# A selective scan and an expert layer on one core: batch 1 routed as one group, tables and rows of zeros moved between the expert slots, a new plan of lagging sums, weights of three experts asked for at once

## The reference, cut to what matters

```python
h = layernorm(x) * (1 + ca) + sa
# scan: x, z, B, C, delta are projections of h; u = silu(conv(x))
def step(h, inp):                      # per channel and state
    dA = exp(dt * A); h = dA * h + (dt * u) * B
    return h, (h * C).sum(-1)
y = (y + u * D) * silu(z)
x = x + ga * (y @ Wout.T + bout)
h = layernorm(x) * (1 + cb) + sb
logits = h @ gate; w, idx = top_k(logits, 2); w = softmax(w)
out = sum over the 2 experts e of w_e * (silu(h @ w0[e]) * (h @ w1[e])) @ wo[e]
x = x + gb * out
```

## Time and profile before

| | |
|---|---|
| median of three runs | 850.11 us |
| profiled execution, its own time | 850.03 us |
| span of that execution | 848.2 us |
| TensorE matmul busy | 737.5 us (87%) |
| VectorE busy | 626.6 us (74%) |
| GpSimd busy | 513.4 us (61%) |
| ScalarE busy | 340.2 us (40%) |
| scan groups end (last sum on TensorE) | 557.0 us |
| first hidden of an expert slot | 600.6 us |

### The profile page before, as it was taken

How to read it: one execution, slowest core, us unless ns; L and a number is a source line. 1 busy time by engine, 2 the same in 40 slices (tenths; PEclk the granted TensorE clock), 3 DMA queues, 4 the chain that set the end, 5 groups by cost and what they waited for, 6 DMA issues and landing times. The chain is left out here.

```text
span 848.2 us, 9598 instructions
## 1 busy us (share of the span) xinstructions
PE 737.5 (87%) x2292; PEld 370.5 (44%) x2293; DVE 626.6 (74%) x840; ACT 340.2 (40%) x387; POOL 513.4 (61%) x271
## 2 busy tenths in 40 slices
PE   5799998888797887878989878986699999999994
PEld 2444343233232332324535323465366666666663
DVE  4478889999899998999999898846444444444442
ACT  0776966456453543545445475311111111111110
POOL 1013233999999999999999898947522222222222
PEclk9999999999999999999999987997599999999998
DMA  9354645866667666676759968567662322222220
GB/s 282 98 158 148 186 158 148 205 183 175 174 158 195 176 175 181 175 188 168 207 159 238 231 138 244 143 238 244 202 203 45 49 45 34 49 46 38 46 30 0
DMA packets 62296, 126.41 MB, mean 149 GB/s; under 512 B 11898, under 2 KB 33850, under 8 KB 62140
## 3 DMA queue, kind: packets, MB, share of 16 engines
q1 hardware_dynamic: 50468, 116.12, 50.0%
q0 software_dynamic: 7152, 8.48, 5.7%
q10 hardware_dynamic: 4648, 1.48, 0.7%
HBM read 98.08 MB, written 24.69 MB: 145 GB/s over the span
## 5 line engine op out<-in xcount | busy, mean ns | idle before, releaser
L1630 POOL TENSOR_TENSOR pool<-pool,hT 128x1024 f32<-128x1024 f32 x101 | 235.8, 2355 | 15.8 <-PE PS L664 15.8
L664 PE MATMUL PS<-pool,ident 128*128 128x512 f32 x404 | 206.3, 637 | 31.0 <-POOL pool L1630 30.2
L1028 ACT ACTIVATE PS<-pool,negA 128x1024 f32<-128x1024 f32 x128 | 143.1, 1118 | 168.3 <-DVE pool L1338 168.3
L1714 POOL DMA_INDIRECT out<-uT,ptab x39 | 60.6, 1555 | 169.1 <-DVE uT L1565 157.9
L1338 DVE TENSOR_TENSOR_SCAN pool<-PS,pool 128x1024 f32<-128x1024 f32 x64 | 143.0, 2270 | 3.4 <-ACT PS L1028 3.4
L849 PE MATMUL PS<-pool,uT 128*128 (+1 forms) x312 | 145.3, 610 | 0.0
L664 PEld LDWEIGHTS PS<-pool,ident 128*128 128x128 f32 x404 | 75.8, 198 | 118.4 <-issue 59.3
L646 PE MATMUL PS<-pool 96*128 96x512 bf16 x256 | 80.8, 398 | 27.9 <-DVE wz_sb L1326 12.0
L1539 DVE TENSOR_TENSOR uT<-uT,PS 128x512 f32<-128x512 f32 x39 | 26.9, 689 | 88.4 <-PE PS L849 85.6
L1654 POOL TENSOR_TENSOR spread<-spread,pool 128x1024 f32<-128x1024 f32 x32 | 75.4, 2355 | 15.3 <-ACT spread L1034 15.3
L849 PEld LDWEIGHTS PS<-pool,uT 128*128 128x128 f32 x312 | 58.3, 197 | 59.0 <-issue 59.0
(11 more groups left out here) (197 smaller groups left out, 867.3 us busy)
## 6 DMA issues: line engine op xcount, KB each, us to landing
hT<-C_scratch SPq DMA_DIRECT2D x128, 512.0 KB, 5.3
pool<-in_w SPq DMA_DIRECT2D x16, 512.0 KB
uT<-expert_in_scratch SPq DMA_DIRECT2D x39, 130.5 KB
Y<-Y SPq DMA_DIRECT2D x32, 128.0 KB, 2.4
C_scratch<-Y SPq DMA_DIRECT2D x8, 512.0 KB, 2.6
pool<-du_scratch SPq DMA_DIRECT2D x8, 512.0 KB, 6.1
Y<-in_wo SPq DMA_DIRECT2D x8, 512.0 KB
expert_in_scratch<-zrow SPq DMA_DIRECT2D x16, 130.5 KB, 5.8
```

Source lines behind the costliest of these rows:

```text
L664: m = pe.matmul(PS[:, 6 + half, :], ident[:, :], prod_k[:, HF * half:HF * half + HF], start=False, stop=k == DS - 1)
L1028: act.activation(pair(2 * (k % 2)).unsqueeze(1), delta[:, chunk_at(g2, r), :], ACT.Exp, scale=decay[:, bass.ds(g2 * (2 * DS) + n, 1)]).the ...
L1630: gp.tensor_tensor(to, hst[:, k % HR, :], crep[k % RC], ALU.mult).then_inc(prod_done, 1)
L1714: gp.indirect_dma_start(out=out, out_offset=bass.IndirectOffsetOnAxis(ap=ptab[:, slot:slot + 1], axis=0), in_=yo[:, slot % 2, :], in_offse ...
```

## The change

It has five parts.

1. `blocks_behind` follows a table, `CATCH_UP`, of the k at which two sums are made. In group 7 the four transposes are made in two pairs (k = 0 and 1), so that the sums begin at k = 2; ScalarE's evacuations stand two each at k = 4 and 5. `first_logits` is one piece at k = 12. `ranks(0)` moves ahead of the last two sums, all `turned_back` behind them.
2. Batch 1 is one group of 8 tiles: one `pick`, `weights`, `ranks` and `place_of`, and 16 sends in a row. `rstd_of(2)` and `rstd_of(3)` stand behind 10 and 15 sends of batch 0 where it was 7 and 13.
3. The tables of later slots are made by VectorE in three pieces, behind `leave` of slots 0, 1 and 2, no longer ahead of slot 0.
4. ScalarE's eight stores of zeros stand in iterations 2 to 5, no longer 0 to 3.
5. SyncE asks for the weights of experts 0 to 2 behind the scan (nine loads, no longer twelve) and for expert e+1's behind the rows of slot e, for e = 2 to 6.

```diff
-GROUPS = ((0, NTB), (NTB, NTB + TQ), (NTB + TQ, NT))
+GROUPS = ((0, NTB), (NTB, NT))
...
             sp.wait_ge(gated, NG - 1)
-            for e in range(CH):
+            for e in range(3):
                 w0_of(e)
                 w1_of(e)
                 wo_of(e)
-            sp.wait_ge(gated, NG)
...
-                if e in (1, 2, 3, 4):
-                    w0_of(e + 3)
-                    if e == 4:
-                        w1_of(e + 3)
-                    wo_of(e + 3)
+                if 2 <= e < NE - 1:
+                    w0_of(e + 1)
+                    if e + 1 < CH or e + 1 == NE - 1:
+                        w1_of(e + 1)
+                    wo_of(e + 1)
...
+            CATCH_UP = {0: (), 2: (4, 6), TQ: (6, 8, 10, 11)}
...
+            def blocks_behind(g2, r, pieces, last):
+                made, behind = 0, len(pieces)
+                sums_at = [0] * behind + [1] * (DS - behind)
+                for k in CATCH_UP[behind]:
+                    sums_at[k] += 1
+                for k in range(DS):
+                    next_front(g2, r, k, last)
+                    if k < behind:
+                        pieces[k]()
+                    if last and k == DS - LAG:
+                        first_logits()
+                    for _ in range(sums_at[k]):
+                        if made == 0:
+                            pair_read(2 * g2 + r)
+                        if last and made == DS - 2:
+                            ranks(0)
+                        back(g2, r, made, prod_at(DS * (2 * g2 + r) + made))
+                        made += 1
...
+            def turned_pair(i):
+                turned_in(2 * i)
+                turned_in(2 * i + 1)
+
+            blocks_behind(NB + 1, 1, [lambda i=i: turned_pair(i) for i in range(2)], True)
+            for j in range(NTB // 2):
+                turned_back(j)
...
-                if g == CH + 3 and k in range(LAG, LAG + NTB // 2):
-                    take_turned(k - LAG)
+                if g == CH + 3 and k in (LAG, LAG + 1):
+                    take_turned(2 * (k - LAG))
+                    take_turned(2 * (k - LAG) + 1)
...
-            act.wait_ge(known, 2)
-            for s2 in range(2):
+            for s2 in range(NE // 2):
                 for r in range(2):
                     take_rows(s2 + 1, r)
                     silu_h(s2 + r, 1 - r)
-                    tail(4 * s2 + 2 * r)
-                    tail(4 * s2 + 2 * r + 1)
-            with act.Fori(2, SPAIRS) as s2:
+                    if s2 in (1, 2):
+                        if s2 == 1 and r == 0:
+                            act.wait_ge(known, 2)
+                        tail(4 * (s2 - 1) + 2 * r)
+                        tail(4 * (s2 - 1) + 2 * r + 1)
+            with act.Fori(NE // 2, SPAIRS) as s2:
...
+            residual(NTB, NTB + TQ)
+            normal_h2(NTB, NTB + TQ)
+            residual(NTB + TQ, NT)
+            normal_h2(NTB + TQ, NT)
             pick(1)
             weights(1)
             place_of(1)
...
-            dve.wait_ge(c_over, 1)
             dve.wait_ge(regated, 1)
...
+            def slots_of(s2, between):
                 for r in range(2):
                     take_inter(s2, r)
                     noted_of(s2 + 1, r)
                     gate_h(s2 + r, 1 - r)
                     leave(s2, r)
+                    if between:
+                        between.pop(0)()
+
+            between = [count_slots, expert_of_slots, rows_of_slots]
+            slots_of(0, between)
+            slots_of(1, between)
+            with dve.Fori(2, SPAIRS) as s2:
+                slots_of(s2, None)
...
-            send(0, slice(0, 7))
+            send(0, slice(0, 10))
             rstd_of(2)
-            send(0, slice(7, 13))
+            send(0, slice(10, 15))
             rstd_of(3)
-            send(0, slice(13, 16))
+            send(0, slice(15, 16))
...
             for q in range(1, NQ):
                 gp.wait_ge(placed, q + 1)
-                send(q, slice(0, 2 * TQ))
+                send(q, slice(0, 2 * NTB))
```

More of the change, by code:

```diff
@@ L711, in turned_back, with first_logits @@
                 m.then_inc(t2_mm, 1)
-            def first_logits(tiles):
-                for t in tiles:
-                    if t == 0:
-                        pe.wait_ge(dbu_done, 1 + NG * OWN)
-                        pe.wait_ge(spread_in, NG * len(SHARED))
-                        pe.wait_ge(t1_done, NTB)
+            def first_logits():
+                pe.wait_ge(dbu_done, 1 + NG * OWN)
+                pe.wait_ge(spread_in, NG * len(SHARED))
+                pe.wait_ge(t1_done, NTB)
+                for t in range(NTB):
                     for k in range(KD):
@@ L722, in first_logits, with ranks @@
                     m.then_inc(g_mm, 1)
+            def ranks(q):
+                first, end = GROUPS[q]
+                n = end - first
+                pe.wait_ge(tables, 1)
+                pe.wait_ge(picked, q + 1)
+                for i in range(n + (q in (0, NQ - 1))):
+                    to = PS[:, r_bank(q), P + NE * i:P + NE * i + NE]
+                    parts = [(ones[:, :], ohs[:, first + j, :]) for j in range(i)]
+                    if q:
+                        parts.append((ones[:, :], sums[:, q, :]))
+                    if i < n:
+                        parts.append((tri[:, :], ohs[:, first + i, :]))
+                    for j, (w, rhs) in enumerate(parts):
+                        m = pe.matmul(to, w, rhs, start=j == 0, stop=j == len(parts) - 1)
+                m.then_inc(rank_mm, 1)
             def next_front(g2, r, k, last):
@@ L772, in _ @@
             blocks_behind(NB + 1, 0, [lambda t=t: outward_y(t) for t in range(TQ, NTB)], False)
-            blocks_behind(NB + 1, 1, [lambda j=j: turned_in(j) for j in range(NTB // 2)], True)
-            turned_back(2)
-            turned_back(3)
+            def turned_pair(i):
[4 more added lines that the diff above has]
+                turned_back(j)
             def turn_h2(t):
@@ L796, in logits @@
                 m.then_inc(g_mm, 1)
-            def ranks(q):
-                first, end = GROUPS[q]
-                n = end - first
-                pe.wait_ge(tables, 1)
-                pe.wait_ge(picked, q + 1)
-                for i in range(n + (q in (0, NQ - 1))):
-                    to = PS[:, r_bank(q), P + NE * i:P + NE * i + NE]
-                    parts = [(ones[:, :], ohs[:, first + j, :]) for j in range(i)]
-                    if q:
-                        parts.append((ones[:, :], sums[:, q, :]))
-                    if i < n:
-                        parts.append((tri[:, :], ohs[:, first + i, :]))
-                    for j, (w, rhs) in enumerate(parts):
-                        m = pe.matmul(to, w, rhs, start=j == 0, stop=j == len(parts) - 1)
-                m.then_inc(rank_mm, 1)
             def scored(q):
@@ L820, in scored @@
                 logits(q, end - 1)
-            ranks(0)
             for t in range(NTB, NT):
@@ L1130, in gap_exp @@
                 act.activation(w12[:, 1, tiles], w12[:, 0, tiles], ACT.Exp).then_inc(ex_done, 1)
-            take_rows2(0)
-            take_rows2(1)
             gap_exp(0)
             leave(NG // 2 - 1, 1)
-            take_rows2(2)
-            take_rows2(3)
+            for j in range(NTB // 2):
+                take_rows2(j)
             for q in range(1, NQ):
@@ L1471, in gate_y, with residual @@
                 dve.tensor_tensor(uT[:, c, :], uT[:, c, :], szT[:, c, :], ALU.mult).then_inc(gated, 1)
-            def residual(q):
-                first, end = GROUPS[q]
+            def residual(first, end):
                 added_y(first)
@@ L1481, in residual, with normal_h2 @@
                     gathered(t)
-            def normal_h2(q):
-                for t in range(*GROUPS[q]):
+            def normal_h2(first, end):
+                for t in range(first, end):
                     centre(t)
-                for t in range(*GROUPS[q]):
+                for t in range(first, end):
                     h2_of(t)
@@ L1575, in _ @@
             gate_h(0, 0)
-            with dve.Fori(0, SPAIRS) as s2:
+            def slots_of(s2, between):
                 for r in range(2):
```

74 lines of the change are left out of this document (31 added, 43 removed).

## The result

The changed kernel took 860.84 us median (858.08 to 862.98, four runs), beside 849.75 us for the kernel before in the same comparison: a ratio of 1.0122, 95% interval 1.0073 to 1.0171. Its profiled execution took 861.73 us, with a span of 859.9 us, 11.7 us more than before. The prediction was 860.0 us with a range of 853.5 to 865.0.

A forecast was written before the change was run, and what follows sets the result against it. TensorE was taken to bound the slots (30% of the span), never waiting from the second slot on. Terms 0 - 0.5 + 2.5 + 0 + 5.5 + 2.5 = +10.0 on 850.03 gave 860.0 us, range 853.5 to 865.0.

The forecast's parts named there:

- The scan's last group: End of the scan: earlier sums but a later front leave GpSimd's input unchanged, about 0, ends -3.5 and +2.5 us.
- the first send stays where it was: Scan to routing: batch 0's rows still wait for four transposes and evacuations behind the last sum; no shift.
- signs of being wrong: Slots without a hole after slot 1, last scan sum over 3 us from 557.0, or a weights hole before slot 2.
- the scan gains: Rival at the scan: early sums free GpSimd, everything up to slot 8 comes 3.5 us earlier, 856.5 us; chance 0.12.
- both waits and a late scan: Rival: GpSimd's input 2.5 us late and both clock drops cost 3.25 us, 864.0 us; chance 0.10.
- Batch 1 as one group: Outward of slot 1: sends start earlier but the last lands at 620.1; start 622.6 against 623.11, -0.5 us.
- The clock: TensorE behind the holes before outward of slot 1 and slot 8: lower granted clock costs 2.5 us each.
- Tables: VectorE between slots: three pieces of 1.2 to 1.6 us, covered by TensorE's hidden except the first, counted elsewhere; 0.
- weights: Expert 3's loads follow slot 2's rows, take 4.5 us and arrive in time; later experts have over 8 us; 0.
- Zeros: Before slot 8: its rows wait for the later stores of zeros, so TensorE stands 5.5 us, ends 4.5 and 6.5.
- Only the sends don't hold: Rival: slot 2's hidden starts about 611.9, not 619.67, while slot 8's hole and clock drop remain; 850.2 us; chance 0.08.
- The early start wins: Rival: the 7.8 us between slots 0 and 2 kept, zeros in time, no hole at slot 8; 842.2 us; chance 0.05.

The follow-up runs named there:

- early zeros: The changed kernel with the zeros' row numbers computed ahead of slot 0 and the eight stores of zeros back in iterations 0 to 3; ratio 1.0141.
- part 1 alone: The kernel before with only the new scan plan (paired transposes, logits in one piece, ranks(0) ahead of the last two sums); ratio 1.0018.
- the version with tables, early buffers and early zeros: The kernel before with later slots' tables made between slots and output buffers freed before batch 1's sends, zeros left in iterations 0 to 3; ratio 0.9943.
- the group alone: The kernel before with only batch 1 routed as one group of 8 tiles, 16 sends in a row, rstd behind 10 and 15 sends; ratio 1.0033.
- part 1 undone: The changed kernel with the old scan plan put back (four single transposes, logits in three parts, batch 0's ranks behind the sums); ratio 1.0146.
- the tables alone: The kernel before with only the tables of later slots made in three pieces behind slots 0, 1 and 2; ratio 0.9963.
- both edits: The changed kernel with output buffers freed before batch 1's sends, and the stores of zeros back in iterations 0 to 3; ratio 1.0106.

## Why the prediction was right

**The sum** was +10.0 and is +11.7; the two holes and the two clock drops are where they were said to be, and behind what they were said to be behind. That the total is so close is in part luck: errors of +2.6 and +0.5 at the first hole stand against -0.7 and -0.6 at the second.

**The scan's last group (about 0).** The step "the first send stays where it was" failed: it came at 565.58, not 561.64. One of the prediction's own signs of being wrong came with it: the last sum of the scan ended at about 561.4, more than 3 us from 557.0. GpSimd's last product ended at 554.06 here and at 552.51 before; the first send followed 11.5 us later, and 9.1 before. Those 2.4 us are the plan's own: GpSimd's idle time in front of the first send is 8.8 us in every profile with the old plan, and 11.2 in four of the five with the new one (9.5 with early zeros). TensorE's timeline of the changed kernel shows where they come from, the last sums and the sums ahead of them:

```profile
550.54 6.25 PE L665 MATMUL PS<-Y,ident 128*128 128x512 f32 x8
557.74 3.68 PE L665 MATMUL PS<-pool,ident 128*128 128x512 f32 x8
```

Eight matmuls that take 3.68 us in the second row took 6.25 in the first, behind the logits in one piece: TensorE lags behind GpSimd's products at a low clock (0.80 over 545 to 562, 0.99 before). With early zeros the same eight took 5.10 and the delay is shorter. No run takes the logits or the clock apart, so this is read from the five profiles and not tested. The prediction looked for the plan's price at GpSimd's input and not at TensorE's sums. The other 1.5 us, by which GpSimd's last product was late, can't be told from the spread of that point (549.8 to 556.3 us in the five profiles with the new plan, 549.4 to 555.4 with the old). The time of part 1 alone can't be told from none. The rival "the scan gains" is excluded by the late first send, "both waits and a late scan" came true in its late scan, but the clock drops cost 3.0 and 1.9 us, not 3.25 each, and the time is 860.84 us, not 864.0.

**Batch 1 as one group (-0.5 at slot 1; it is +2.1).** The distance from the first send of batch 0 to that of the last group was put 2.9 us shorter and is 4.1 shorter (35.24 against 39.31); the late scan of 3.9 us takes all of it, so the sends start at 600.82 instead of 598.0. The last of them starts at 619.87, not 617.5, and has landed 3.2 us later, not 2.6: the wait ends at 623.1 where 620.1 was said. What stands behind the wait was put at 2.4 us and took 2.2.

**The clock (+2.5 twice)** is +3.0 and +1.9: the drop behind the hole of 7.5 us costs more than behind that of 4.8.

**Tables (0) and weights (0).** In the change they cost nothing in the sum beyond `count_slots`, which is in its first term. The weights do show: slot 3's rows, asked for at 605.04 behind expert 3's loads, were turned at 613.51, after an idle time of TensorE of 1.21 us, but TensorE stood until 625.33 all the same. That both lie in the shadow of the sends is argued, since no run took one of them out of the changed kernel; alone in the kernel before, tables gained 0.37% and weights cost 0.23%.

**Zeros (+5.5; it is +4.8).** From the issue of the last pair to the turn of slot 8 it took 7.5 us (650.56 to 658.07) where 8.0 was said. The two transfers took 2.92 and 2.25 us against 2.7 and 2.95 in the sum. The figure of the Trainium skill ("DMA: Bandwidth & Descriptors", Anatomy of one DMA), fitted there for DMAs that GpSimd issues, is an estimated 2.3 us for these 134 KB. The trace agrees for the rows (2.25) and not for the zeros (2.92), and the hole that follows from it, 4.5 us, is nearer to the measured 4.8 than mine.

**Rivals.** "Only the sends don't hold" fell: the sends hold even with the buffers given free early. "The scan gains" fell with the first send. "The early start wins" asked for sends that don't hold and zeros in time; the change has neither, and the version with tables, early buffers and early zeros, which has both, is faster than before.

## What to carry to other kernels

Fewer, larger groups save fixed steps (3.5 us in the group alone) and lengthen the block that one in-order queue must issue: look for what stands behind that block, and who waits for it. Removing a wait on a buffer helps only if the instruction that empties the buffer isn't queued behind the same block: it did with eight sends in front, and moved the hole by two slots with sixteen. A store that a later read waits for has a due time, so move it only within the cover that the trace shows.

## What the runs showed of the hardware

Transfers of the same 134 KB of rows took 2.02 us with no weight load in front of them and 8.13 us behind 1.5 MB of weights, at 336 GB/s and a DMA share of 0.99 (2.10 and 6.77 us in the second profile of that kernel). Indirect sends were issued 1.27 us apart, so that sixteen hold GpSimd's queue for some 20 us. The last send of batch 1 had landed 2.7 and 3.2 us after its issue began in two profiles (part 1 undone, the change) and 5.1 to 8.1 us after it in six others (5.1 with early zeros, 7.1 with the tables alone, 8.1 with both edits). The two quick ones fell where the transfers in progress were running out (DMA share 0.29 in 612 to 618 with part 1 undone, 0.26 in 621 to 623 in the change); in the tables' profile the stretch of 612 to 618 had a share of 1.06 and 392 GB/s. Early zeros show that it isn't enough to count the weights asked for at the time: the last load had been asked for at 609.15, 8.9 us ahead of the send, much as in the change (9.9), but ScalarE had asked for two stores of zeros at 615.04, and the DMA engines were still at a share of 1.04 and 351 GB/s in 618 to 621. No run took weights or zeros away there, so that the load is the cause is argued, not shown.
